# A channel-norm gate kernel: 50 buffers and 34 kept tiles instead of 49 and 33, and a load plan with other constants

## The reference

```
g   = (x - mean_group) / sqrt(var_group + 1e-5)       # 32 groups of 4 channels, over all pixels of the batch
u,s = mean and standard deviation of g over the 128 channels, per pixel (ddof = 1)
n   = W @ ((g - u) / (s + 1e-6)) + b                  # a 128 x 128 product per pixel
out = x + g * n                                       # x is the input, before any normalisation
```

## Time and profile before

| | |
|---|---|
| median of 3 runs | 1960.63 us (1960.15 to 1963.23) |
| the profiled execution | 1957.16 us, its span 1955.4 us |
| busy: PE, VectorE, ScalarE, GpSimd | 88%, 92%, 74%, 75% |
| moved by DMA | 671.63 MB, mean 343 GB/s |
| loads, stores of tiles | 760 and 512 of 512 KB |

### The profile page before, as it was taken

The page is one execution under the profiler, slowest core; times in us unless marked ns, Lnnn a source line. Parts: engine busy times, 40 slices in busy tenths (PEclk is TensorE's granted clock), DMA queues, the critical chain, the costliest instruction groups (busy, mean ns, idle before and its releaser), DMA issues.

```text
span 1955.4 us, 67613 instructions
## 1 busy us (share of the span) xinstructions
PE 1713.4 (88%) x28706; PEld 922.9 (47%) x28706; DVE 1803.2 (92%) x2120; ACT 1440.7 (74%) x2498; POOL 1460.6 (75%) x1684
## 2 busy tenths in 40 slices
PE   0079997999889998999989999899988999899997
PEld 0045554555445554455545554455544555455553
DVE  5669999999999998999989998999989999898988
ACT  5598885888768885788858888588876888544442
POOL 0077877878778886788868787787877888688885
PEclk9989999999999999999999999999999999999999
DMA  9989998999989998999989999899998999854775
GB/s 379 390 308 337 388 377 291 402 378 377 337 293 415 372 385 322 338 396 373 387 303 378 372 385 350 304 406 373 380 346 310 401 364 384 315 196 185 270 258 218
DMA packets 184188, 671.63 MB, mean 343 GB/s; under 512 B 20688, under 2 KB 21072, under 8 KB 183888
## 3 DMA queue, kind: packets, MB, share of 16 engines
q1 hardware_dynamic: 110160, 398.85, 55.0%
q10 hardware_dynamic: 73728, 268.47, 34.6%
HBM read 398.80 MB, written 268.44 MB: 341 GB/s over the span
## 4 chain that ended last, share of the span: by engine, by line
PE 47%; DVE 27%; issue 9%; DMA 9%; POOL 3%; SPq 2%; ACT 2%; POOLq 0%; ACTq 0%; DVEq 0%
PE proj_ps L734 28%; PE sums_ps L722 10%; DVE scaled L632 9%; PE factor_ps L708 9%; DMA tiles<-x 6%; DVE tiles L645 6%; DVE bn L676 4%; DVE bn L677 4%; DMA out<-tiles 3%; SPq L408 2%; POOL tiles L441 1%; POOL tiles L452 1%; DVE var L651 1%; ACT unused L509 1%; DVE gn L580 1%
## 5 line engine op out<-in xcount | busy, mean ns | idle before, releaser
L734 PE MATMUL proj_ps<-scaled,w_t 128*32 128x512 f32 x8192 | 992.3, 602 | 0.1
L452 POOL TENSOR_SCALAR tiles<-tiles,out_shift 128x1024 f32<-128x1024 f32 x512 | 576.8, 1127 | 228.6 <-DVE tiles L645 214.9
L645 DVE SCALAR_TENSOR_TENSOR tiles<-proj_ps,gate_shift,tiles 128x1024 f32<-128x1024 f32 x512 | 643.2, 1256 | 46.4 <-PE proj_ps L734 46.0
L441 POOL TENSOR_SCALAR tiles<-tiles,norm_scalars 128x1024 f32<-128x1024 f32 x512 | 618.6, 1208 | 58.0 <-DMA tiles<-x 57.2
L509 ACT ACTIVATE unused<-tiles,bn 128x1024 uint8<-128x1024 f32 x560 | 636.5, 1137 | 2.5 <-issue 1.7
L632 DVE TENSOR_TENSOR scaled<-tiles,factor_ps 128x1024 f32<-128x1024 f32 x512 | 618.4, 1208 | 6.1 <-PE factor_ps L708 3.8
L524 ACT ACTIVATE squares<-tiles 128x1024 f32<-128x1024 f32 x512 | 539.0, 1053 | 99.1 <-POOL tiles L441 74.2
L708 PE MATMUL factor_ps<-pieces,pick_sb 128*128 128x128 bf16 x4096 | 319.8, 221 | 130.5 <-DVE scaled L632 111.5
L722 PEld LDWEIGHTS sums_ps<-tiles,const_sb 128*32 128x32 f32 x8192 | 245.6, 111 | 317.9 <-issue 283.7
L734 PEld LDWEIGHTS proj_ps<-scaled,w_t 128*32 128x32 f32 x8192 | 214.7, 109 | 365.0 <-issue 311.5
L708 PEld LDWEIGHTS factor_ps<-pieces,pick_sb 128*128 128x128 bf16 x4096 | 232.5, 98 | 245.8 <-DVE scaled L632 164.5
(11 more groups left out here) (56 smaller groups left out, 679.9 us busy)
## 6 DMA issues: line engine op xcount, KB each, us to landing
tiles<-x SPq DMA_DIRECT2D x760, 512.0 KB, 9.7
out<-tiles ACTq DMA_DIRECT2D x512, 512.0 KB, 6.9
const_sb<-const SPq DMA_DIRECT2D x1, 193.5 KB, 2.3
scaled<-w SPq DMA_DIRECT2D x1, 64.0 KB, 2.1
scaled<-ident SPq DMA_DIRECT2D x1, 64.0 KB, 2.1
pick_sb<-pick SPq DMA_DIRECT2D x1, 8.0 KB, 2.2
bias_sb<-bias SPq DMA_DIRECT2D x1, 0.5 KB, 2.3
```

Of the source, the lines that this page charges most:

```text
L441: nc.gpsimd.tensor_scalar(place(s), place(s), norm_scalars[:, 0:1], norm_scalars[:, 1:2], ALU.add, ALU.mult).then_inc(normed, 1)
L452: nc.gpsimd.tensor_scalar(place(s), place(s), 1.0, out_shift[:, 0:1], ALU.mult, ALU.add).then_inc(finished, 1)
L645: nc.vector.scalar_tensor_tensor(out=place(s), in0=proj_ps[:, s % 2, :], scalar=gate_shift[:, 0:1], in1=place(s), op0=ALU.add, op1=ALU.mul ...
L734: mm = nc.tensor.matmul(proj_ps[q:q + 32, s % 2, h:h + BANK], w_t[:, q:q + 32], scaled[:, s % 2, h:h + BANK], start=True, stop=True)
```

## The change

Six edits. BUFFERS goes from 49 to 50 and KEPT from 33 to 34. STORE_STEPS goes from 1 to 2 and LOAD_GAP from 0.62 to 0.64. To find the room, the eight stationary operands of L722 (8 x 32 columns) become eight windows of one array of 40 columns. Their start moves by one column each. `miss` becomes another name of `root`, with a wait on the ScalarE queue between L529 and the squaring of the root, which now writes over its input. Six small columns share one array, and the scratch for dynamic DMAs is declared smaller.

```
-BUFFERS = 49
-KEPT = 33
+BUFFERS = 50
+KEPT = 34
...
-STORE_STEPS = 1
+STORE_STEPS = 2
 DROP_STEPS = 2
-LOAD_GAP = 0.62
+LOAD_GAP = 0.64
...
-CONST_COLS = {"group_avg": P, "sum_rows": ROWS * 32, "rows_bc": 1, "rows_c": 1, "norm_eps": 1}
+CONST_COLS = {"group_avg": P, "sum_rows": ROWS + 32, "rows_bc": 1, "rows_c": 1, "norm_eps": 1}
...
-        "sum_rows": np.tile(np.arange(32)[None] % ROWS == np.arange(ROWS)[:, None], (P, 1, 1)).reshape(P, -1),
+        "sum_rows": np.tile(np.arange(ROWS + 32) % ROWS == 0, (P, 1)),
...
-        bias_sb = sb("bias_sb", [P, 1])
-        w_sum = sb("w_sum", [P, 1])
+        columns_sb = sb("columns_sb", [P, 8])
+        bias_sb, w_sum, gate_shift, out_shift = (columns_sb[:, i:i + 1] for i in range(4))
+        norm_scalars = columns_sb[:, 4:6]
...
-        miss = sb("miss", [P, CHUNK])
+        miss = root
...
                         nc.scalar.add(approx[:, :], root[:, :], at["norm_eps"]).then_inc(root_eps_done, 1)
+                        act.wait_ge(root_eps_done, done)
                         nc.scalar.activation(miss[:, :], root[:, :], ACT.Square).then_inc(root_sq_done, 1)
...
-                        rows = at["sum_rows"][:, 32 * k:32 * k + 32]
+                        rows = at["sum_rows"][:, ROWS - k:ROWS - k + 32]
...
-    nc = bacc.Bacc("TRN2", target_bir_lowering=False, num_devices=1, dynamic_dma_scratch_size=1024)
+    nc = bacc.Bacc("TRN2", target_bir_lowering=False, num_devices=1, dynamic_dma_scratch_size=256)
```

More of the change, by code:

```diff
@@ L236, in norm_gate_kernel @@
         new_scalars = sb("new_scalars", [P, 4])
-        norm_scalars = sb("norm_scalars", [P, 2])
-        gate_shift = sb("gate_shift", [P, 1])
-        out_shift = sb("out_shift", [P, 1])
         sum_sq = sb("sum_sq", [P, CHUNK])
```

## The result

The changed kernel takes **1931.93 us** (median of 6 runs, 1930.15 to 1936.15) against 1960.39 us (6 runs, 1951.43 to 1963.23) for the kernel before. The ratio is 0.9867, with a 95% interval of 0.9844 to 0.9890. The forecast was 1935.6 us, 25.0 us less than before. The ratio says 26 us less, with an interval of 22 to 31; the two medians lie 28.5 us apart.

A forecast was written before the change was run, and what follows sets the result against it. VectorE was taken as the fullest engine, held up by late loads at period ends, with TensorE bounding the last period. -24.7 - 0.3 = -25.0 us from the median 1960.63 gave 1935.6 us, range 1930 to 1944.

The forecast's parts named there:

- What was lost, and where: Late loads cost 25.9 us in steps 54 to 58 of seven middle periods, 2.26 us in the last period.
- The cause: Loads at period ends wait for stores to free their buffers; the plan's three steps were 2.9 us short.
- The chain in microseconds: Store issue to norm: four steps, 13.7 us, for 11.4 to 12.7 by medians; usual load 1 to 2.3 us early.
- The three signs of being wrong: Steps 46 to 53 not 27.4 us, load waits moving into first steps, or peak load rate below 417 GB/s.
- KEPT 34 and LOAD_GAP 0.64 at nothing: Stream loads: 4.2 MB fewer and a slower pace, costed at 0 as lying beside VectorE's work.
- The bytes rival: If 363 GB/s is all a period gets, only 4.2 MB count: 11.5 us, 1949 us; chance 0.09.
- The slower stores rival: Stores slow down with the longer queue; half way, 12 to 13 us won, 1948 us; chance 0.13.
- The shifted weight loads and the ScalarE wait at nothing: TensorE's weight loads stay at 111 ns; ScalarE's 0.1 us wait is covered by the reciprocal's; both 0 us.
- The -0.3 us for smaller constants: At the start, the constants' transfer is 0.11 MB smaller at 417 GB/s, saving 0.3 us.
- the stretch from step 59 on: Period ends: up to 1.4 us more could come back; taken as 0, group scalars counted as VectorE work.
- The main term: Late loads at period ends: -24.7 us of 28.2 us lost, leaving 0.5 us per middle period.

The follow-up runs named there:

- b1: Changed kernel with KEPT 33, STORE_STEPS 3 and LOAD_GAP 0.62, 50 buffers kept: 1932.33 us, 0.9853 of the kernel before.
- a2_store2: Changed kernel with BUFFERS 49, KEPT 33 and LOAD_GAP 0.62 put back, STORE_STEPS 2 kept: 1934.18 us, 0.9869 of the kernel before.
- a1_old_plan: Changed kernel with all four old constants (49, 33, STORE_STEPS 1, 0.62), only the layout edits left: 1963.17 us, 1.0007 of the kernel before.
- b3: Changed kernel with BUFFERS 49, KEPT 33, STORE_STEPS 0 and LOAD_GAP 0.62: 1988.23 us, 1.0130 of the kernel before.
- a3: Changed kernel with STORE_STEPS 1 and LOAD_GAP 0.62 put back, 50 buffers and KEPT 34 kept: 1956.31 us, 0.9977 of the kernel before.
- b2_warm: Changed kernel plus 8 overwritten matmuls on TensorE at steps 60 and 63 of each period: 1923.81 us, 0.9809 of the kernel before.
- b0: The changed kernel run again unchanged, for comparison in its group: 1931.50 us, 0.9847 of the kernel before.
- c1_before_warm: Kernel before plus only the 8 added matmuls at steps 60 and 63: 1953.92 us, 0.9967 of the kernel before.
- b4_store3_warm: Changed kernel with KEPT 33, STORE_STEPS 3, LOAD_GAP 0.62 and the 8 added matmuls at steps 60 and 63: 1923.23 us, 0.9808 of the kernel before.

## Why the prediction was right

- **What was lost, and where.** The forecast took 25.9 us of loss in steps 54 to 58 and 2.26 in the last period. After, 111.9 us stand there for 136.0, so 24.1 came back and 1.9 were left, for the 3.5 that I had left. b1, without any late load, has 109.7, so the undisturbed value of 110.04 was right to 0.4 us. In the last period steps 56 to 63 got back 2.3 us, as worked out. This term was right, against the trace that it was read from.
- **The cause.** One step more from store to load. a2_store2 against a1_old_plan is that constant alone, and it gives all of it. b1 and b3 give the dose, with nothing more to win at three steps.
- **The chain in microseconds.** The direction was right, and the margin smaller than forecast. Four steps were counted as 13.7 us from the store's issue to the norm; an undelayed norm starts 12.8 us after it. The store and the load of slot 57 took 11.3 to 12.9 us in the middle periods, for the 11.4 to 12.7 worked out from the medians. So the usual load, forecast 1 to 2.3 us early, was 0 to 1.5 us early, and a few short waits remained.
- **The three signs of being wrong** did not come: steps 46 to 53 still take 27.4 us, no wait for a load moved into the first steps, and 20 us in mid-period (836 to 856) still run at 418 GB/s.
- **KEPT 34 and LOAD_GAP 0.64 at nothing.** Right on top of the longer chain: a2 without them has the gain of the whole change. Wrong as a statement about them alone: a3 gained 4.5 us. The two gains don't add up. That they are the same waits is likely, and not shown.
- **The bytes rival** is ruled out by a2, which moves all the bytes of before in 0.9869 of the time. The changed kernel moves 364 GB/s over a period. The Trainium skill ("DMA: Bandwidth & Descriptors", "Where 436 GB/s comes from") gives some 358 GB/s as what binds a core between HBM and SBUF; it did not bind here.
- **The slower stores rival.** Over the seven middle periods the median store issued in steps 44 to 53 took 7.5 us to landing, before and after, and in steps 54 to 63 5.8 us before and 5.3 after. The stores did not get slower.
- **The shifted weight loads and the ScalarE wait at nothing.** 111 ns as before, and a1 at 1.0007 for all layout edits together. The 0.1 us of delay was right as well: it stands in the cover of L457, 0.10 us per chain, and the chain behind it waits for VectorE as before.
- **The -0.3 us for smaller constants** was mis-sized. That transfer did get shorter, by 0.4 us. But VectorE and TensorE begin when the last of five small loads has landed, and that came at 4.78 us after 4.88, so 0.1 us was won. It can't be seen in the total.
- **What the working missed.** I left the stretch from step 59 on out, with up to 1.4 us there, and called it the work of VectorE. It holds more: b2_warm sums to 362.0 us there and the kernel before to 369.0. After the change it got longer, not shorter, by 3.8 us in this profile and 2.6 in b0's, with 8 falls for 6 in both. So the profiled execution gained only 21.1 us of span: 24.1 in steps 54 to 58 and 2.3 in the last period, less 3.8 in steps 59 to 7, 1.2 ahead of the first multiply and 0.3 at the very end. In b0's profile the span gained 24.3.
- **Where luck helped.** The losses were read from an execution of the kernel before that was 3 us faster than its median, and taken off the median. A slower one, that of a1_old_plan with the same plan (1960.30 us), lost 5.3 us in steps 56 to 63 of the last period and not 2.3. So the usual execution probably had more to win than the forecast counted, and what it missed from step 59 on took about as much away. The 25.0 us match the measured 26 in part for this reason, as far as two traces of the old plan can tell. The main term does not depend on it.

Still open is which of the gaps brings a fall and which doesn't, and whether LOAD_GAP 0.64 is worth anything by itself.

## What to carry to other kernels

Where a planner hands a buffer from a store to a load, add up the chain in real time, from the store's issue to its landing, from the load's issue to its landing, and compare it with the time that the plan allows. Take both from the trace: the allowed time is what passes from the store's issue to a use that waits for nothing, and the landing times change with what else is in flight. Here three steps, some 10 us, were allowed for a chain of 13, and one constant was worth 1.3%. The way to find such a loss under an engine that is 95% busy is to take the differences of one instruction's starts, step by step over several periods, and to look for the steps that don't repeat.

## What the runs showed that I had not expected

- Gaps of 2.2 to 2.5 us on TensorE, in a stream that is 93% busy, were followed by a granted clock of 1.2 GHz in some periods, at 0.7 to 0.9 us of a period for one fall and 2.6 us for two (b1_store3: 53.1 and 53.4 us with one, 55.1 with two, 52.5 with none). Eight matmuls that nobody reads, 2.05 us of work at each of two places, took 7.7 us off a kernel whose fullest engine is VectorE.
- With the added matmuls the time also spreads less. The nine runs of c1_before_warm lie within 3.5 us (1951.79 to 1955.31), while the fourteen of the kernel before beside them ran from 1953.59 to 1966.06. b4_store3_warm lies within 0.8 us, and b1_store3, the same without the matmuls, within 1.7. This fits the falls as one source of the spread; the traces don't show it directly.
